# A low part moved from GpSimd to VectorE, and a cap from VectorE to ScalarE, in a four-layer graph network

## The reference

```python
# layer 0: scores (xW1)(xW2)^T, leaky relu, mask, softmax, times xW3, relu
# layer 1: h = xW, scores s1_i + s2_j, leaky relu, mask, softmax, times h, elu
# layer 2:
out = relu(x @ mlp1_w + mlp1_b)                    # 512 features
residual = out
out = elu(_gat(out, None, W_fc, a_fc)) + residual  # no mask: the "unmasked layer"
out = relu(out @ mlp2_w + mlp2_b)
out = relu(elu(_gat(out, adj, W_hand, a_hand)) + out)
# layer 3: four-head attention with mask, softmax, output projection
```

## Time and profile before

| | us |
|---|---|
| median of 3 runs | 2623.06 (2622.87 to 2627.22) |
| the profiled execution | 2623.28 |
| its span in the trace | 2621.5 |
| TensorE busy | 2492.3, 95% of the span |
| VectorE busy | 2250.0, 86% |
| ScalarE busy | 1967.4, 75% |
| GpSimd busy | 1913.3, 73% |

### The profile page before, as it was taken

The page is one execution under the profiler, slowest core; times in us unless marked ns, Lnnn a source line. Parts: engine busy times, 40 slices in busy tenths (PEclk is TensorE's granted clock), DMA queues, the critical chain, the costliest instruction groups (busy, mean ns, idle before and its releaser), DMA issues.

```text
span 2621.5 us, 63997 instructions
## 1 busy us (share of the span) xinstructions
PE 2492.3 (95%) x21064; PEld 2379.1 (91%) x21064; DVE 2250.0 (86%) x6252; ACT 1967.4 (75%) x4737; POOL 1913.3 (73%) x2439
## 2 busy tenths in 40 slices
PE   5789999999999999999999999999999999999973
PEld 4789999999999999999999999999999999998862
DVE  3478899889999999998998999999889989998874
ACT  2468877887887788778878877887887788787642
POOL 2457777877787877778787777878777787777542
PEclk8899999999999999999999999999999999999986
DMA  4214444444444444444443444444444444443333
GB/s 142 66 52 125 131 141 128 128 138 129 134 125 145 127 126 141 130 137 125 143 129 123 137 135 133 128 139 130 131 128 142 128 127 139 129 137 108 103 101 89
DMA packets 317112, 329.63 MB, mean 126 GB/s; under 512 B 35312, under 2 KB 248688, under 8 KB 316784
## 3 DMA queue, kind: packets, MB, share of 16 engines
q1 hardware_dynamic: 316784, 325.54, 41.4%
HBM read 174.41 MB, written 150.99 MB: 124 GB/s over the span
## 4 chain that ended last, share of the span: by engine, by line
PE 88%; DVE 5%; DMA 2%; POOL 2%; ACT 1%; issue 1%; SPq 1%; POOLq 0%; DVEq 0%; ACTq 0%
PE ps L288 60%; PE ps L407 6%; PE ps L406 6%; PE ps L520 4%; PE ps L494 4%; PE ps L298 3%; PE ps L304 2%; PE ps L434 1%; POOL p L1210 1%; DMA scratch_pro<-act 1%; DVE p L1100 1%; SPq L245 0%; DMA scratch_o<-sco 0%; DVE o2T_lo L784 0%; DVE act L925 0%
## 5 line engine op out<-in xcount | busy, mean ns | idle before, releaser
L1210 POOL TENSOR_TENSOR p<-p,rd 128x512 f32<-128x512 f32 x256 | 342.6, 1348 | 5.5
L1135 POOL TENSOR_TENSOR proT_lo<-sco,proT_hi 128x512 fp32r<-128x512 f32 x128 | 166.1, 1297 | 163.9 <-ACT proT_hi L536 163.9
L1147 POOL TENSOR_SCALAR xn<-act,nmean,rstd 128x256 f32<-128x256 f32 x384 | 237.0, 626 | 47.7 <-DVE act L1051 35.4
L762 ACT ACTIVATE p<-p,nmx 128x256 f32<-128x256 f32 x512 | 252.8, 496 | 10.9 <-DVE nmx L1085 10.9
L549 ACT ACTIVATE sco<-sco,nmax 128x256 f32<-128x256 f32 x384 | 192.4, 502 | 43.1 <-DVE nmax L848 38.4
L1157 POOL TENSOR_TENSOR act<-act,x 128x512 f32<-128x512 f32 x64 | 83.2, 1300 | 167.9 <-ACT act L599 167.9
L1085 DVE CUSTOM_DVE_ANT_0 p<-ps,mask 128x256 f32<-128x256 f32 x512 | 188.3, 414 | 15.3 <-PE ps L494 13.8
L848 DVE CUSTOM_DVE_ANT_0 sco<-ps,mask 128x256 f32<-128x256 f32 x384 | 145.0, 415 | 53.7 <-ACT ps L539 39.4
L784 DVE TENSOR_TENSOR xnT_lo<-ps,xnT_hi 128x512 fp32r<-128x512 f32 x192 | 129.7, 676 | 61.7 <-ACT xnT_hi L536 61.7
L1142 POOL TENSOR_TENSOR rstd<-vare,mhalf 128x2 f32<-128x2 f32 x256 | 178.0, 695 | 0.0
L1100 DVE STREAM_TRANSPOSE p<-p 128x1024 f32<-128x1024 f32 x128 | 158.6, 1239 | 19.1 <-POOL p L1210 18.6
(11 more groups left out here) (238 smaller groups left out, 12345.4 us busy)
## 6 DMA issues: line engine op xcount, KB each, us to landing
scratch<-p SPq DMA_DIRECT2D x128, 512.0 KB, 3.0
p4T<-scratch SPq DMA_DIRECT2D x512, 128.0 KB, 3.5
scratch_pro<-act SPq DMA_DIRECT2D x192, 256.0 KB, 2.3
sco<-scratch_pro SPq DMA_DIRECT2D x768, 64.0 KB, 1.9
x0Tp<-in_xT SPq DMA_DIRECT2D x64, 256.0 KB, 2.6
x<-in_x SPq DMA_DIRECT2D x64, 256.0 KB, 2.8
scratch_o<-sco SPq DMA_DIRECT2D x64, 256.0 KB, 2.1
o3r<-scratch_o SPq DMA_DIRECT2D x256, 64.0 KB, 2.4
```

The source lines that it names most:

```text
L762: ins = nc.scalar.activation(rows_, rows_, ACT.Exp, scale=-1.0, bias=nmx4[:, h, m:m + 1], accum_out=den4[:, h, m:m + 1])
L1135: return G.tensor_tensor(lo, whole, hi.bitcast(fp32), ALU.subtract)
L1147: ins = G.tensor_scalar(xn[:, m, :], y[:, m, :], nmean[i][:, m:m + 1], rstd[i][:, m:m + 1], ALU.add, ALU.mult)
L1210: G.tensor_tensor(rows_, rows_, rd4[:, h, :].unsqueeze(2).unsqueeze(3).broadcast_to([P, NT, QUADS, CT * QP]), ALU.mult).then_inc(S["p4n"], 1)
```

## The change

Three edits. First, `m2`, the low part of `o1T`, is issued by VectorE instead of GpSimd, with the same operands and semaphores. Second, the cap goes to ScalarE. `y2` makes `relu(-att)` instead of `exp(att)`, a new step `b2` makes `exp(-ex2)` of it, which is `exp(min(att, 0))`, that is `min(exp(att), 1)`, and `k2` follows as before. VectorE's `n2` goes; its `i2`, which overwrites `att`, now waits for the relu instead of the exponential. Third, all five lists are new; the diff shows TensorE's.

```diff
-    "pe": "x0:2 d2:5 v4:7 n2:4 s40:7 w2:5 v2:5 s42:7 a1:3 h1:2 c2:4 g0:0 a0:1 a3:6 f1:2 r2:4 h0:0 m3:5 s0:0 x1:3 f2:4 a4:7 x3:6 m2:3 y4:7 h3:5 q4:6 k4:6 f3:5",
+    "pe": "f3:6 d2:5 x0:2 v4:7 n2:4 s40:7 v2:5 w2:5 s42:7 a1:3 h1:2 g0:0 a3:6 a0:1 c2:4 f1:2 h0:0 r2:4 m3:5 s0:0 f2:4 x1:3 a4:7 x3:6 m2:3 y4:7 h3:5 q4:6 k4:6",
...
 
             def y2(t):
                 ac.wait_ge(S["att"], t + 1)
-                nc.scalar.activation(ex2[:, :, :], att[:, :, :], ACT.Exp).then_inc(S["ex1"], 1)
+                nc.scalar.activation(ex2[:, :, :], att[:, :, :], ACT.Relu, scale=-1.0).then_inc(S["cut2"], 1)
+
+            def n2b(t):
+                ac.wait_ge(S["cut2"], t + 1)
+                nc.scalar.activation(ex2[:, :, :], ex2[:, :, :], ACT.Exp, scale=-1.0).then_inc(S["ex1"], 1)
 
             def k2(t):
-                ac.wait_ge(S["cut2"], t + 1)
+                ac.wait_ge(S["ex1"], t + 1)
                 nc.scalar.activation(ex2[:, :, :], ex2[:, :, :], ACT.Exp, bias=W["m1"][:, 0, 0:1]).then_inc(S["ex2"], 1)
 
             def z2(t):
...
 
+            def m2(t):
+                dv.wait_ge(S["o1Th"], t + 1)
+                low_part(o1Tp, o1T[t % 2][:, :, :]).then_inc(S["o1Tl"], 1)
+
             def hidden_low(m):
                 def step(t):
                     dv.wait_ge(S["hfch"], 2 * t + m + 1)
...
 
-            def n2(t):
-                dv.wait_ge(S["ex1"], t + 1)
-                V.tensor_scalar(ex2[:, :, :], ex2[:, :, :], 1.0, None, ALU.min).then_inc(S["cut2"], 1)
-
             def i2(t):
-                dv.wait_ge(S["ex1"], t + 1)
+                dv.wait_ge(S["cut2"], t + 1)
                 V.scalar_tensor_tensor(att[:, :, :], att[:, :, :], 0.0, o1T[t % 2][:, :, :], ALU.max, ALU.add).then_inc(S["res"], 1)
 
             def j2(t):
...
 
-            def m2(t):
-                po.wait_ge(S["o1Th"], t + 1)
-                low_part(o1Tp[1][:, :, :], o1T[t % 2][:, :, :], o1Tp[0][:, :, :]).then_inc(S["o1Tl"], 1)
-
             def w2(t):
                 po.wait_ge(S["pfch"], t + 1)
                 low_part(pfcp[1][:, :, :], pfc[:, :, :], pfcp[0][:, :, :]).then_inc(S["pfcl"], 1)
```

More of the change, by code:

```diff
@@ L773, in _ @@
                        "h1": h1_, "u1": u1, "p1": p1, "t1": t1, "a1": a1, "x1": x1_,
-                       "m2": half(0), "n2": half(1), "o2": o2, "c2": hidden_high(0), "r2": hidden_high(1), "f2": f2, "w2": w2, "x2": x2, "y2": y2, "k2": k2, "z2": z2,
+                       "m2": half(0), "n2": half(1), "o2": o2, "c2": hidden_high(0), "r2": hidden_high(1), "f2": f2, "w2": w2, "x2": x2, "y2": y2, "b2": n2b, "k2": k2, "z2": z2,
                        "m3": m3, "o3": o3, "h3": h3_, "u3": u3, "p3": p3, "t3": t3, "a3": a3, "b3": b3, "x3": x3_,
@@ L1119, in _ @@
             run("dv", {"g0": g0, "h0": h0_, "e0": e0, "i0": i0, "t0": t0, "st0": st0, "ag0": ag0, "x0": x0_, "h1": h1_, "e1": e1, "i1": i1, "t1": t1, "b1": b1, "a1": a1, "st1": st1, "ag1": ag1, "x1": x1_,
-                       "c2": hidden_low(0), "r2": hidden_low(1), "f2": f2, "b2": b2, "d2": d2, "q2": q2, "rb2": b2_, "v2": v2, "n2": n2, "i2": i2, "j2": j2, "z2": z2,
+                       "m2": m2, "c2": hidden_low(0), "r2": hidden_low(1), "f2": f2, "b2": b2, "d2": d2, "q2": q2, "rb2": b2_, "v2": v2, "i2": i2, "j2": j2, "z2": z2,
                        "o3": o3, "h3": h3_, "e3": e3, "i3": i3, "t3": t3, "c3": c3, "b3": b3, "a3": a3, "r3": r3, "z3": z3, "st3": st3, "ag3": ag3, "x3": x3_,
@@ L1234, in t3 @@
                 low_of_turned(proT[2], 2).then_inc(S["proT2"], 1)
-            run("po", {"l0": l0, "t0": t0, "t1": t1, "t3": t3, "a0": a0, "v0": v0, "n0": n0, "y1": y1, "v1": v1, "n1": n1, "m2": m2, "w2": w2, "m3": m3, "v3": v3, "n3": n3, "k4": k4,
+            run("po", {"l0": l0, "t0": t0, "t1": t1, "t3": t3, "a0": a0, "v0": v0, "n0": n0, "y1": y1, "v1": v1, "n1": n1, "w2": w2, "m3": m3, "v3": v3, "n3": n3, "k4": k4,
                        "p40": p4_(0), "p41": p4_(1), "p42": p4_(2), "p43": p4_(3),
```

## The result

The changed kernel took 2702.05 us (median of 4 runs, 2697.59 to 2705.44) against 2623.85 for the kernel before on the same chip: 1.0302 times as long, interval 1.0289 to 1.0315. The forecast was 2635, with 2656 as its upper end. The sign was right and the size was not: 78 us instead of 12. The profiled execution has a span of 2695.7 us, 74.2 more than the 2621.5 of before.

A forecast was written before the change was run, and what follows sets the result against it. TensorE, saturated through the middle, was taken as the bound. Profiled 2623.3 + 17 (wait at `a3`, 57 rounds) - 2.8 (filling) - 2.5 (emptying) = 2635 us; own range 2625 to 2652, 8 in 10 from 2612 to 2656.

The forecast's parts named there:

- `r2`: TensorE step: in the filling, `h0` ahead of it fills its gap, 1.4 us saved; no cost in the middle's rounds.
- filling: Start of the run: gaps ahead of `r2` and `s0` close, 1.4 us each, -2.8 us; bounds -7 to +2.
- emptying: End of the run: GpSimd's `p42` and `p43` no longer run together, -2 us; taken as -2.5, bounds -7 to +4.
- The chain to `a3`: TensorE's `a1` over ScalarE and GpSimd's `t3` to `a3`: 2.94 us against 2.81 of cover; with restart 0.24 a round.
- blocked `t3`: GpSimd's `t3` held on SBUF by VectorE's `b1`, ending 0.21 us later: 0.45 us a round instead of 0.24; taken 0.30.
- Times 57 rounds: The 0.30 us a round at `a3`, paid in rounds 7 to 63: 17 us, 0 to 34.
- The other edge of `a3`: Bank 3, freed by VectorE's `a1` about 2.7 us after `h1`'s start against TensorE's 2.81: adds nothing, no room left.
- Rival 3: GpSimd's `t3` gets SBUF ahead of VectorE's `b1` and delays `a3`: 1.5 us a round, 86 us, 2704; chance 0.04.
- The ends: Filling and emptying, where waits count: -2.8 and -2.5 us.
- The edits as work: Low part to VectorE at 1.22 us, cap to ScalarE at 1.06: cost nothing in the middle, hidden by TensorE's saturation.
- rival 2: VectorE becomes the bound, short by 0.8 us a round: 46 us, 2664; chance 0.13.
- Rival 1: The wait at `a3` never shows, rounds stay 38.09 us and only the ends act: 2618; chance 0.33.

The follow-up runs named there:

- experiment 5: The changed kernel's new orders with the code of the kernel before (low part on GpSimd, cap on VectorE): 2802.92 us, ratio 1.0693 to the kernel before.
- experiment 8: Changed kernel with GpSimd's `t3` cut from 128x512 to 128x32, that part of the computation left out: 2668.37 us, ratio 1.0172 to the kernel before.
- 7: Changed kernel with ScalarE's `t3` ahead of its `a1`, as in the kernel before: 2755.24 us, ratio 1.0512 to the kernel before.
- Experiment 9: Changed kernel with VectorE's low part of `c2` cut from 128x512 to 128x64, the rest left zero: 2677.70 us, ratio 1.0209 to the kernel before.
- experiment 2: Kernel before, old orders, with only the cap moved to ScalarE: 2627.83 us, ratio 1.002.
- experiment 3: Kernel before, old orders, with only the low part moved to VectorE and the cap still there: 2751.22 us, ratio 1.049.
- experiment 4: Both code edits in the old orders, with VectorE's `m2` ahead of `x0`, about 4 us earlier: 2639.40 us, ratio 1.0067 to the kernel before.
- 6: Changed kernel with `a0` ahead of `a3` on TensorE: 2742.69 us, ratio 1.0453 to the kernel before.
- 10: Changed kernel with SyncE's list of transfers from the kernel before: 2868.41 us, ratio 1.0935 to the kernel before.
- 11: Changed kernel with `c2` back between `h1` and `g0`, ScalarE and VectorE adapted, VectorE's `m2` ahead of `x0`: 2957.91 us, ratio 1.1275.
- 12: Changed kernel with `c2` back between `h1` and `g0`, ScalarE and VectorE adapted, VectorE's `m2` behind `v2`: 2842.36 us, ratio 1.0834.

## Why the prediction was wrong

Where the 74.2 us of the span went, from the lengths of TensorE's steps, 56 rounds each (mean after less mean before):

| step | forecast a round | measured a round | 56 rounds |
|---|---|---|---|
| wait of `a3`, seen in `g0` | 0.19 | 0.57: 0.38 plain, the rest in 21 rounds | 32.1 |
| restart of `a3` | 0.11 | 0.11 | 5.9 |
| `h0` to `r2`, with `f1` and `r2` | 0 | 0.26 | 14.7 |
| all other steps (`v4` +0.16, `f3` to `x0` -0.08) | 0 | 0.07 | 4.1 |
| filling | -2.8 in all | | +6.3 |
| emptying | -2.5 in all | | +11.2 |

The forecast's sum was 62.5 us short of this: 10.4 for the plain size of the wait at `a3` (56 times 0.49 for 17), 10.6 for its spread, 14.7 for `r2`, 4.1 for the other steps and 22.8 for the ends (rounding leaves 0.1).

*The chain to `a3`.* Right as a mechanism, and shown: it is in the changed kernel's waits, it came with the new lists under the old code (experiment 5), and cutting GpSimd's part of it gave 34 us back (experiment 8). Its plain size, 0.49 with the restart, lies at the forecast's 0.45 for a blocked `t3`; I took 0.30 as a mean of blocked and free, and the block came in the plain rounds too.

*Its spread.* "Times 57 rounds" failed by itself (it is 56 rounds, but that is only 0.3 us). I worked out the chain once, from typical durations, and took it for every round. A wait at the end of a chain without slack isn't symmetric: what is early gains nothing, what is late is paid in full. The 21 rounds with more than the plain wait add the 10.6 us. About 6.8 of them are the five rounds in which GpSimd came first, and 3.4 the nine with a late transfer. Late transfers had been there before, and cost nothing (38.07 against 38.09).

*The other edge of `a3`.* "There is no room left either" was right: bank 3 stood 0.16 us behind (experiment 8), took over when ScalarE's order was turned (7), and was 1.4 to 1.8 us late in the five rounds in which GpSimd came first. Rival 3, as a matter of every round, had a chance of 0.04; it holds in one round of eleven, and its 2704 us beside the measured 2702 are chance.

*`r2`.* I said of the filling that `h0` ahead of `r2` fills the gap, and put nothing down for the middle. It fills 1.39 of 1.60 us. Before, `g0`, `a0` and `a3` stood there too, 4.2 us. This step of the prediction was wrong in kind: I had looked at what the new lists put ahead of `a3`, and not at what they put ahead of the second half of the step that they moved. Experiment 9 shows it, 24 us with the ends. In the nine rounds with a late transfer and one other the gap is 0.48 longer still.

*The ends.* The largest part: credited -5.3, measured +17.5. I counted the gaps that I had seen and that would close, and not that the two new chains lose their cover there: `proT_lo` +8.1 and `hfc_lo` +5.1 us in the emptying. Of the gaps of the filling that I had counted, the waits ahead of `r2` fell by 1.0 us and those ahead of `s0` by 1.4; other waits grew by more, and TensorE was busy 4.5 us longer at the lower clock. Of the 2 us for GpSimd's `p42` and `p43` little came: they run apart now, but VectorE's second transposition ends 7.8 us behind the start of the last `s42`, where it was 8.2. The cuts of experiments 8 and 9, each in its own run, take 9.7 and 7.4 us off the ends.

*The edits as work.* "Costs and gives nothing in the middle" holds for a plain round with the cap (experiment 2, 5 us in all) but not for both, even with `m2` early: a plain round is 0.24 longer there, and the 16 us are more than the whole slowdown of 12 that I had forecast. The low part isn't 1.22 but 1.49 us where GpSimd is at work beside it. Without its partner the same edit costs 128 us (experiment 3). There VectorE's list is what TensorE waits for, as in rival 2.

*Rival 1*, that the wait never shows, is out.

`v4`'s +0.16 is two things. In a plain round it is 0.10, at its first matmuls: `x0` and `d2` have changed places, so `v4` now follows `x0`'s transpositions. The same exchange made `f3` 0.08 shorter. The rest is the waits of `n2` behind it, 3.8 us in nine of the 56 rounds after and 1.8 in two before.

What stays open: 34 and 24 us of the 78 are shown by cutting a step each, and the rest is read from the step lengths alone. What made the granted clock of the filling lower isn't shown, and whether another order of the new lists would do with both edits what experiment 4 does wasn't tried. No version was faster than the kernel before: there its rounds are 38.01 us with TensorE at work all through, and nothing in these edits shortens that.

## What to carry to other kernels

Where an engine is full, ask of each of its waits not whether it is covered but by how much, and compare the slack with the spread of what is waited for: the 4.1 us ahead of `a3` had absorbed late transfers that nobody saw, and with none the nine that reached ScalarE's `t3` were paid. When a step is moved, recount the cover of both its sides, and of its second half. And an order is tuned as a whole: five changes to the new lists, each sensible by itself (experiments 6, 7, 10, 11 and 12), made it 1.5 to 9.5% slower still.
